# The class row's six additions per pair move from GpSimd to VectorE in an audio tower kernel (tokeniser, selective scan, mixture of experts)

## The reference, cut to what matters

```python
h = tok(x)                         # forward + backward EWMA over time, 128 -> 256 projection + bias
# two selective-scan layers on layernorm(h); per layer:
#   delta = softplus(x @ Wd + bd); u = x @ Wi + bi; decay = exp(-delta * softplus(A_log))
#   state_t = decay_t * state_{t-1} + delta_t * u_t;  y = states @ Wo + bo
#   class_state = final_state @ Ws + bs;  hidden = y + class_state[:, None, :]
h = h + hidden_after_layer_2       # y and the class row are both added to the token rows
# mixture of experts on layernorm(h): shared SwiGLU (512 wide), 16 routed experts (4 groups, top 4)
h = h + shared(xn) + routed(xn)
```

## Time and profile before

| | |
|---|---|
| median of 3 executions | 1364.24 us (1349.87 to 1368.43) |
| the profiled execution | 1353.63 us |
| its span, first to last instruction | 1351.8 us |
| mean granted TensorE clock | 0.926 of full speed |
| busy: TensorE / VectorE / ScalarE / GpSimd | 1192.3 / 943.9 / 549.4 / 479.7 us |

### The profile page before, as it was taken

The page is one execution under the profiler, slowest core; times in us unless marked ns, Lnnn a source line. Parts: engine busy times, 40 slices in busy tenths (PEclk is TensorE's granted clock), DMA queues, the critical chain, the costliest instruction groups (busy, mean ns, idle before and its releaser), DMA issues.

```text
span 1351.8 us, 24750 instructions
## 1 busy us (share of the span) xinstructions
PE 1192.3 (88%) x7477; PEld 1075.1 (80%) x7477; DVE 943.9 (70%) x2326; ACT 549.4 (41%) x899; POOL 479.7 (35%) x329
## 2 busy tenths in 40 slices
PE   4469859978999799977999899977999899999997
PEld 3358648768987689866988789867988789899997
DVE  6886996986479865897578864797658763654443
ACT  1525623622455235432366235452355343223332
POOL 2053382153315432164403623173412712163333
PEclk8659878988999899998999899997899899999999
DMA  3230021022323112231222303231122312244331
GB/s 105 47 86 23 28 83 31 27 74 56 51 41 88 44 22 47 40 93 48 25 63 57 88 10 52 40 93 41 13 48 39 90 37 24 42 125 71 51 52 21
DMA packets 88288, 71.48 MB, mean 53 GB/s; under 512 B 39671, under 2 KB 82848, under 8 KB 88168
## 3 DMA queue, kind: packets, MB, share of 16 engines
q1 hardware_dynamic: 58832, 43.30, 11.9%
q0 software_dynamic: 26832, 26.06, 11.7%
q10 hardware_dynamic: 2504, 0.55, 0.2%
HBM read 31.36 MB, written 39.34 MB: 52 GB/s over the span
## 4 chain that ended last, share of the span: by engine, by line
PE 62%; DVE 14%; issue 10%; POOL 9%; ACT 4%; DMA 0%; POOLq 0%; ACTq 0%; DVEq 0%
PE gu_ps L1669 18%; PE gu_ps L1642 13%; PE d_ps L1729 9%; PE d_ps L1710 7%; POOL lists L767 4%; PE ch_ps L1619 3%; PE ch_ps L1697 3%; PE ch_ps L1550 2%; POOL h L764 2%; PE ch_ps L1689 1%; PE ch_ps L1568 1%; DVE states L1157 1%; PE ch_ps L1610 1%; POOL out_dram L786 1%; PE ch_ps L1580 1%
## 5 line engine op out<-in xcount | busy, mean ns | idle before, releaser
L786 POOL DMA_INDIRECT out_dram<-block_rows,entry x99 | 160.3, 1619 | 323.4 <-ACT block_rows L926 271.7
L1669 PE MATMUL gu_ps<-gu_hi,bx_hi 128*128 x792 | 247.0, 312 | 15.3 <-issue 15.2
L914 ACT ACTIVATE hid<-gu_ps 128x512 f32<-128x512 f32 (+1 forms) x195 | 115.0, 592 | 301.3 <-PE gu_ps L1669 207.5
L1669 PE MATMUL gu_ps<-gu_lo,bx_hi 128*128 x792 | 232.1, 293 | 0.0
L1669 PE MATMUL gu_ps<-gu_hi,bx_lo 128*128 x792 | 231.7, 293 | 0.0
L767 POOL DMA_INDIRECT lists<-records,pos x96 | 139.5, 1453 | 196.1 <-DVE pos L1338 170.6
L1710 PE MATMUL d_ps<-down,hid 128*125 128x256 f32 x768 | 188.8, 391 | 0.0
L1669 PEld LDWEIGHTS gu_ps<-gu_hi,bx_hi 128*128 128x128 f32 x792 | 158.3, 200 | 24.7 <-issue 23.3
L1710 PEld LDWEIGHTS d_ps<-down,hid 128*125 128x125 f32 x768 | 144.5, 196 | 20.3 <-issue 0.3
L1669 PEld LDWEIGHTS gu_ps<-gu_hi,bx_lo 128*128 128x128 f32 x792 | 159.2, 201 | 1.2
L1669 PEld LDWEIGHTS gu_ps<-gu_lo,bx_hi 128*128 128x128 f32 x792 | 158.1, 200 | 0.0
(11 more groups left out here) (279 smaller groups left out, 2922.1 us busy)
## 6 DMA issues: line engine op xcount, KB each, us to landing
block_rows<-lists SPq DMA_DIRECT2D x99, 128.0 KB, 4.7
out_dram<-h SPq DMA_DIRECT2D x24, 500.0 KB
t<-rstd_scratch SPq DMA_DIRECT2D x21, 250.0 KB, 4.8
x_in<-in_x_dram SPq DMA_DIRECT2D x8, 375.0 KB, 7.8
zt<-in_x_dram SPq DMA_DIRECT2D x7, 375.0 KB, 3.9
entry<-lists SPq DMA_DIRECT2D x99, 8.0 KB, 3.0
out_dram<-block_rows,entry POOLq DMA_INDIRECT x99, 3.9
lists<-records,pos POOLq DMA_INDIRECT x96, 4.4
```

Source lines behind the costliest of these rows:

```text
L786: pool.indirect_dma_start(out=out_rows[0:there, :], out_offset=bass.IndirectOffsetOnAxis(entry[n % UE][:, ID:ID + 1].bitcast(U32), 0), in_ ...
L914: inc(act.activation(hid[g % 4][:, 0:n], gu_ps[:, 2 * (g % 2), 0:n], ACT.Silu), "silu_done")
L1669: last = pe.matmul(gu_ps[:, 2 * (g % 2) + half, q * GH:(q + 1) * GH], a[n % 2][:, k, :], w[:, k, bass.ds(of, 1), half * GH:(half + 1) * GH ...
```

## The change

The step "residual" leaves GpSimd's list and comes into VectorE's, with the same operation, operands and wait. On VectorE each residual stands directly ahead of the y of the same tiles. Beside it the timetable is changed in small ways; the lines that the prediction speaks of:

```diff
-    ("ewma", 0, dict(SP=-32.5, DVE=-33.5, POOL=-29.0, ACT=-28.5)),
+    ("ewma", 0, dict(SP=-32.5, DVE=-33.5, POOL=-29.0, ACT=-29.0)),
-    ("ewma", 1, dict(SP=-27.0, DVE=-28.5, POOL=-27.0, ACT=-26.5)),
+    ("ewma", 1, dict(SP=-27.0, DVE=-28.5, POOL=-27.0, ACT=-27.0)),
-    ("spread", 0, dict(SP=-21.5)),
+    ("spread", 0, dict(SP=-19.5)),
-    ("residual", 0, dict(POOL=-6.5)),
-    ("residual", 1, dict(POOL=-6.5)),
-    ("residual", 2, dict(POOL=-6.5)),
-    ("residual", 3, dict(POOL=-5.5)),
-    ("split", (1, 0), dict(ACT=-8.0, DVE=-7.0)),
+    ("split", (1, 0), dict(ACT=-8.0, DVE=-7.5)),
     ("class_row", 0, dict(PE=-7.0, DVE=-7.5)),
-    ("residual", 4, dict(POOL=-2.5)),
     ("split", (1, 1), dict(ACT=-6.5, DVE=-7.0)),
-    ("residual", 5, dict(POOL=-1.5)),
+    ("residual", 0, dict(DVE=-5.5)),
     ("y", (0, 0), dict(PE=-5.5, DVE=-5.5)),
+    ("residual", 1, dict(DVE=-4.5)),
     ("y", (0, 1), dict(PE=-5.0, DVE=-4.5)),
     ("ln2_stats", 0, dict(DVE=-4.5, POOL=-4.0)),
+    ("residual", 2, dict(DVE=-4.5)),
     ("y", (1, 0), dict(PE=-4.5, DVE=-4.5)),
-    ("ln2_norm", 0, dict(DVE=-4.0, ACT=-3.5)),
+    ("ln2_norm", 0, dict(DVE=-4.0, ACT=-4.0)),
+    ("residual", 3, dict(DVE=-4.0)),
     ("y", (1, 1), dict(PE=-4.0, DVE=-4.0)),
...
+    ("residual", 4, dict(DVE=-1.5)),
     ("y", (2, 0), dict(PE=-1.5, DVE=-1.5)),
...
+    ("residual", 5, dict(DVE=-0.5)),
+    ("y", (2, 1), dict(PE=-0.5, DVE=-0.5)),
...
-    ("list", 9, dict(POOL=19.5)),
-    ("list", 10, dict(POOL=19.5)),
-    ("list", 11, dict(POOL=19.5)),
+    ("list", 9, dict(POOL=18.0)),
+    ("list", 10, dict(POOL=21.5)),
+    ("list", 11, dict(POOL=21.5)),
...
@@ gpsimd
-                elif step == "residual":
-                    wait(pool, "row_ev", pair + 1)
-                    hv = h_of[pair % 2][:, 2 * arg:2 * arg + 2, :]
-                    row = rows[:, arg // 3, :].unsqueeze(1).broadcast_to([TP, 2, D])
-                    inc(pool.tensor_tensor(hv, hv, row, ALU.add), "res_done")
@@ vector
+                elif step == "residual":
+                    wait(dve, "row_ev", pair + 1)
+                    hv = h_of[pair % 2][:, 2 * arg:2 * arg + 2, :]
+                    inc(dve.tensor_tensor(hv, hv, rows[:, arg // 3, :].unsqueeze(1).broadcast_to([TP, 2, D]), ALU.add),
+                        "res_done")
```

More of the change, by code:

```diff
@@ L83 @@
     ("route_order", 0, dict(DVE=7.5)),
[L84 removed]
     ("place_hot", 0, dict(DVE=9.0)),
     ("place", 0, dict(PE=10.5, DVE=10.0)),
+    ("logit", 1, dict(PE=2.0, DVE=2.0)),
     ("score_exp", 0, dict(ACT=5.0)),
     ("route_groups", 0, dict(DVE=7.5)),
+    ("route_groups", 1, dict(DVE=7.5)),
+    ("route_top", 0, dict(DVE=11.0)),
     ("place_groups", 0, dict(DVE=9.0)),
[L90 to L91 removed]
     ("route_marks", 0, dict(DVE=12.0)),
@@ L126 @@
     (1, "table", 3): dict(DVE=19.5),
-    (1, "list", 11): dict(POOL=21.5),
+    (1, "list", 11): dict(POOL=21.0),
     (1, "list", 6): dict(POOL=16.5),
@@ L139 @@
     (1, "x2t", (0, 1)): dict(ACT=-3.5),
-    (0, "residual", 4): dict(POOL=-1.5),
-    (0, "residual", 5): dict(POOL=-1.5),
     (0, "ln2_stats", 0): dict(POOL=-3.5),
-    (0, "ln2_stats", 1): dict(POOL=-3.0),
+    (0, "ln2_stats", 1): dict(POOL=-3.5),
     (0, "ln2_stats", 2): dict(POOL=-1.0),
-    (0, "list", 7): dict(POOL=17.0),
-    (0, "list", 6): dict(POOL=21.0),
+    (0, "list", 7): dict(POOL=17.5),
+    (0, "list", 6): dict(POOL=21.5),
     (0, "list", 9): dict(POOL=17.5),
@@ L152 @@
     (1, "route_weights", 0): dict(DVE=13.0),
-    (0, "list", 3): dict(POOL=16.0),
-    (0, "list", 4): dict(POOL=17.0),
-    (0, "list", 5): dict(POOL=19.0),
+    (0, "list", 3): dict(POOL=16.5),
+    (0, "list", 4): dict(POOL=17.5),
+    (0, "list", 5): dict(POOL=19.5),
     (1, "list", 10): dict(POOL=20.5),
@@ L159 @@
     (0, "list", 11): dict(POOL=19.0),
-    (1, "list", 1): dict(POOL=11.5),
-    (1, "list", 2): dict(POOL=12.5),
-    (1, "list", 3): dict(POOL=13.0),
+    (1, "list", 1): dict(POOL=10.5),
+    (1, "list", 2): dict(POOL=11.5),
+    (1, "list", 3): dict(POOL=12.0),
     (1, "list", 4): dict(POOL=14.0),
@@ L168 @@
     (0, "x2t", (0, 0)): dict(ACT=-3.5),
-    (2, "list", 11): dict(POOL=20.5),
+    (2, "list", 11): dict(POOL=18.5),
+    (1, "list", 9): dict(POOL=18.5),
+    (1, "ewma_back", 0): dict(DVE=-32.5),
+    (1, "pre", (1, 1)): dict(PE=-11.0, DVE=-11.0, ACT=-10.5),
+    (1, "ssm_scan", 0): dict(DVE=-15.0),
+    (1, "pre", (1, 0)): dict(DVE=-13.0),
+    (1, "score_exp", 0): dict(ACT=5.5),
+    (0, "spread", 0): dict(SP=-19.5),
+    (1, "list", 0): dict(POOL=11.5),
+    (1, "spread", 0): dict(SP=-26.0),
+    (0, "split", (1, 0)): dict(ACT=-6.5, DVE=-8.0),
+    (1, "rstd_row", 1): dict(PE=-23.5),
+    (0, "carry", 0): dict(DVE=-14.0),
+    (0, "ewma", 1): dict(SP=-24.0),
+    (0, "pre", (1, 0)): dict(DVE=-13.0),
+    (0, "pre", (1, 1)): dict(DVE=-12.5),
+    (0, "ssm_decay", 1): dict(DVE=-10.0),
+    (0, "pre", (1, 2)): dict(DVE=-12.0),
+    (0, "ssm_scan", 1): dict(DVE=-9.5),
+    (0, "ssm_log", 1): dict(DVE=-11.0),
+    (0, "class_row", 0): dict(DVE=-8.0),
+    (0, "split", (1, 1)): dict(DVE=-7.5),
+    (1, "ln2_stats", 0): dict(POOL=-3.0),
+    (1, "ln2_stats", 1): dict(POOL=-1.0),
+    (1, "ln2_stats", 2): dict(POOL=-0.5),
+    (1, "residual", 5): dict(DVE=-1.5),
 }
@@ L174 @@
     (-32.2, "tokw", 0),
-    (-28.0, "tokw", 1),
+    (-30.0, "tokw", 1),
     (-23.9, "tokw", 2),
@@ L189 @@
     (-11.9, "shared", 2),
-    (-11.4, "shared", 3),
+    (-11.9, "shared", 3),
     (8.4, "routed", 3),
     (-10.7, "shared", 4),
-    (10.4, "routed", 4),
+    (8.4, "routed", 4),
     (11.4, "routed", 5),
     (-6.7, "shared", 5),
-    (-11.5, "routed_loads", 0),
+    (-12.5, "routed_loads", 0),
     (-8.5, "routed_loads", 1),
-    (-7.5, "routed_loads", 2),
+    (-6.5, "routed_loads", 2),
     (-6.5, "routed_loads", 3),
-    (-5.5, "routed_loads", 4),
+    (-7.5, "routed_loads", 4),
     (-4.5, "routed_loads", 5),
```

56 lines of the change are left out of this document (26 added, 30 removed).

## The result

| | before | changed |
|---|---|---|
| median of runs (us) | 1358.07 (1349.87 to 1368.43, 4 runs) | 1319.05 (1317.08 to 1321.9, 4 runs) |
| profiled execution: time / span (us) | 1353.6 / 1351.8 | 1317.1 / 1314.9 |
| granted TensorE clock | 0.926 | 0.943 |

The ratio is 0.9693, with a 95% interval of 0.9646 to 0.974: faster by 3.1%. The forecast was 1352 us with a range from 1326 to 1376. It had the direction, and the time lies outside the range.

The account below looks back on a forecast made before the run. It took the loss to lie in about 30 us of each pair, where GpSimd's additions lock VectorE out of SBUF and TensorE waits. 10 + 6 + 1.5 + 2 + 1 - 10.9 = 9.6 us gained, leaned to 1352 us; range 1326 to 1376.

Parts of the forecast that it names:

- Part 2: VectorE's split of the last states, held by GpSimd's back-to-back additions: 10 us gained, bounds 0 and 19.
- Other entries move by half a tick among work that waits for TensorE: 0: Remaining half-tick timetable moves, among work waiting for TensorE: 0, bound 5 us either way.
- Parts 3 and 4: Shorter GpSimd queue before rstd, 6 us, and y's wait, 1.5; split (1, 0) ahead of class_row, 2; earlier ew_hi, 1.
- Part 3: List writes moved from in front of rstd shorten nmr and its waits: 6 us, bounds 0 and 12; y's wait 1.5.
- ew_hi: ScalarE's ew_hi half a tick earlier gives GpSimd ew_lo sooner: 1 us gained, between 0 and 3.
- the split's place: Split (1, 0) ahead of class_row on VectorE, filling the wait for L1596: 2 us gained, 7.4 at most.
- Part 5: VectorE's 48 new additions at 0.68 us: residuals 2 and 3 on the path, 10.9 us lost, others hidden; bounds 0, 32.6.
- Numbers 0 and 1: Residuals 0 and 1 of a pair, in front of y on VectorE: hidden in its waits, the second barely.
- Rival B: VectorE paces the stage and its additions are held themselves: 24 us lost, 1388 us, chance 0.12.
- Rival A: TensorE becomes the stage's limit, holds count at full price, VectorE's additions mostly hide: 37 us gained, 1327 us, chance 0.22.
- Rival C: The split is held again, by list writes and fw in a row: no gain, 1364 us, chance 0.18.
- The signs named ahead: Trace marks: right if split under 3 us, nmr under 300 ns; wrong if additions' mean over 1 us, split held 5.

Follow-up runs that it names:

- e11: Kernel before with all list writes at the new ticks, plus two unread VectorE reductions ahead of the split in pairs 4, 5 and 6: 1354.5 us, ratio 0.998.
- e12: Changed kernel with VectorE's additions 0 and 1 of each pair one tick earlier: 1308.5 us, ratio 0.964 to before.
- e9: Kernel before with only list writes 10 and 11 of a pair moved behind rstd, to tick 21.5: 1340.1 us, ratio 0.987.
- e18: Old timetable without the six additions (class row missing), with all list writes at the new ticks: 1300.7 us, 18.6 under the same without moved list writes.
- e6: Kernel before, additions on GpSimd, with only all list writes at the changed kernel's ticks: 1326.5 us.
- e5: Kernel before, additions on GpSimd, with only ScalarE's ew_hi half a tick earlier: 16 us gained.
- e7: Kernel before, additions on GpSimd, with only VectorE's split (1, 0) moved ahead of its class_row: 12 us gained by the medians.
- the crossed runs: Ratios to before: new timetable, GpSimd additions 0.963; old timetable, VectorE additions 0.976; no additions (class row missing), old timetable 0.970, new 0.949.

## Why the prediction was wrong

**Part 2, the held split, was mis-priced, and this is the step whose reasoning fell.** The forecast said that a hold of 7.4 us "costs 3.1 us of progress, since the next window catches up on part of it". It costs nearly its length: e11 put 30 us in and 28 to 31 came out, and e12 took 7.8 us of hold out and 10.5 us went. The reading failed in its measure. Busy work in three fixed windows is not time: the 3.1 us are work at full clock, in a stage where TensorE does 0.7 us of it per microsecond, and the windows start 5.3 us behind the class row in pair 4 and 3.9 us behind it in pair 5. At equal work the same trace had the full price: pairs 4 and 6 took 47.4 and 47.1 us for the 200 matmuls in which pair 5 took 39.6. The reference was disturbed as well, by the list writes in front of rstd and nmr's 1.76 us: the changed kernel takes 35.1 to 35.7 us for them. The split's whole hold in the profiled execution is 24.5 us, so part 2 was worth 20 to 25 us by that price, and not 10; the forecast's upper bound was 19. It also overlooked the hold of 5.4 us in pair 7, which fell on `table` right ahead of the split.

**"Other entries move by half a tick among work that waits for TensorE: 0", with 5 us as the bound, was the larger miss.** Parts 3 and 4 and this sentence made 9 us of the timetable. It was worth 30 without any addition and 49 with GpSimd's. Part 3's mechanism (list writes in front of rstd) was right and its size was not: 6 us, bound 12, against 18 in e9, 18.6 in e18 and 32 for all list writes in e6. It counted nmr's own time and wait, which fell from 15.6 to 11.3 us, and not the later start of the transposes behind it. ew_hi, priced at 1 with a bound of 3, measured some 15 in e5 (4 to 25 by the interval); the split's place, priced at 2 with a bound of 7.4, some 12 in e7 (8 to 16). The entries also act by which pairs' splits meet GpSimd's row, which the forecast took as given in three pairs. A tenth of a microsecond decides over 7.4 us, three times a run. For ew_hi this is the smaller part, as its pair 4, held like that of before, is 5.7 us shorter; for the split's place the part is open.

**Part 5 was right in its duration (0.684 us for 0.68) and in the rule that 2 and 3 cost and 4 and 5 are hidden** (8.7 us for 10.9; 2.5 for 0), but the 8.7 lie mostly in the first pairs and not spread over eight. Numbers 0 and 1 were called hidden; they took about 8 us in e12, and in the changed kernel another 10.5 for meeting fw and ew_lo. In all 30 us in place of 10.9, close to the bound of 32.6.

**Rival B's mechanism was there and its outcome not.** The additions were held, "one of them a pair", 9.4 us for the 14 forecast, and the wait of y for TensorE went from 17.6 us to 8.4. The two large gains it left out outweighed it. Rival A's time, 1327, is 8 us above the measurement, by luck: its holds at full price were right in kind, but it had 20.5 us for GpSimd's additions, which cost 40, 22 for the timetable, which gave 30, and VectorE's additions at 5 us, which cost 30, and these errors cancel. Rival C did not occur: the split was never held for more than 0.8 us.

Put together from the crossed runs: GpSimd's additions leave (-40), the timetable without additions (-30), VectorE's additions come (+30): 1359 - 40 = 1319. The forecast had 11.5, 9 and 10.9 for these three.

**The signs named ahead** nearly all came as "right": split under 3 us, nmr under 300 ns, the wait for the split under 10, TensorE at 20 or more of 30 us (23.7 to 24.0 from the class row on in pairs 3 to 6, 21.3 in pair 2). They described the mechanism and did not test the prices. The one that would have, a mean over 1 us for the additions, stayed just below at 879 ns.

**What stays open.** Beyond the smaller holds, e6 and e9 won 15 to 18 us each in the presence of GpSimd's additions, and e18 four beyond holds and waits without them. The list writes' place is the cause, since nothing else was changed; the steps from rstd to the transposes are seen to come earlier with them, but no run priced one of these steps by itself. The other 11 us of the 30 that the timetable is worth without additions were not taken apart, nor was what holds leave unexplained of the 9 and 30 us of VectorE's additions.

## What to carry to other kernels

Price a delay of an engine that paces a stage at its full length until a run says otherwise, and compare a disturbed stage with one that is shown to be undisturbed in everything, at equal work (the time to the same matmul) and not in equal windows. A hold that is gone from one operation may have moved to the one ahead of it, so sum them over the whole engine. When a change comes with a new timetable, each moved entry in an engine's in-order queue is an edit of its own: here three groups of them gave as much by themselves as the edit that gave the change its name, and crossing the two halves in four runs showed it at once. Where engines exclude each other, ask for the gap between their operations in the trace: if it is a fraction of a microsecond, any edit in front of it can turn a hold on or off.
